# Preparation of a selective-scan kernel re-placed over 51 scan steps, a first tile with homes of its own, and identity matmuls ahead of the scans

## What is computed

```python
deltaBC = einsum('bld,od->blo', x, W_bc)          # x is normalised
dt_r, Bm, Cm = deltaBC[..., :64], deltaBC[..., 64:96], deltaBC[..., 96:]
delta = softplus(einsum('blr,dr->bld', dt_r, W_dt) + b_dt)
def step(h, inp):                                  # over 1024 time steps
    dA  = exp(delta_t[:, :, None] * A[None])       # A = -exp(A_log)
    dBu = (delta_t * u_t)[:, :, None] * B_t[:, None, :]
    h   = dA * h + dBu                             # h: (batch 4, 256, state 32)
    y_t = einsum('bdn,bn->bd', h, C_t)
y = scan(step) + u * D_param
```

## Time and profile before

| | us |
|---|---|
| median of 3 runs | 1049.39 (1044.85 to 1049.46) |
| the profiled execution | 1052.26 |
| its span, first to last instruction | 1050.3 |
| mean granted TensorE clock in it | 0.807 |

### The profile page before, as it was taken

How to read it: one execution, slowest core, us unless ns; L and a number is a source line. 1 busy time by engine, 2 the same in 40 slices (tenths; PEclk the granted TensorE clock), 3 DMA queues, 4 the chain that set the end, 5 groups by cost and what they waited for, 6 DMA issues and landing times.

```text
span 1050.3 us, 22285 instructions
## 1 busy us (share of the span) xinstructions
PE 868.0 (83%) x7468; PEld 633.2 (60%) x7468; DVE 767.9 (73%) x774; ACT 507.6 (48%) x897; POOL 459.7 (44%) x779
## 2 busy tenths in 40 slices
PE   5324798599979997899789978999999987999994
PEld 3114566466657665666566655666666655787883
DVE  7602697578657865786579658868999994889884
ACT  3451376347534753474347435754555514454441
POOL 6530435254425442545243525444333462555634
PEclk9655698869666967696669668967999978999998
DMA  7869356734663467356734573466646535210011
GB/s 297 92 132 145 52 104 90 157 54 96 89 151 58 96 81 157 60 96 86 148 61 99 81 156 59 102 87 144 95 96 99 112 96 148 63 61 21 21 41 61
DMA packets 234658, 103.59 MB, mean 99 GB/s; under 512 B 168112, under 2 KB 226992, under 8 KB 234160
## 3 DMA queue, kind: packets, MB, share of 16 engines
q1 hardware_dynamic: 234112, 95.80, 48.4%
q10 hardware_dynamic: 432, 6.29, 1.4%
HBM read 58.43 MB, written 43.61 MB: 97 GB/s over the span
## 4 chain that ended last, share of the span: by engine, by line
PE 39%; issue 25%; DVE 14%; POOL 7%; SPq 6%; ACT 5%; DMA 2%; ACTq 0%; POOLq 0%; DVEq 0%
DVE arena L1755 9%; PE psum L1339 7%; PE psum L1400 7%; PE psum L1407 7%; PE psum L1327 7%; PE psum L428 5%; PE psum L1260 2%; POOL arena L369 2%; POOL carry L1210 2%; SPq L945 1%; ACT arena L1558 1%; POOL arena L360 1%; SPq L970 1%; SPq L924 1%; PE psum L497 1%
## 5 line engine op out<-in xcount | busy, mean ns | idle before, releaser
L1755 DVE TENSOR_TENSOR_SCAN arena<-arena,psum 128x1024 f32<-128x1024 f32 x256 | 573.2, 2276 | 195.0 <-PE psum L1407 169.4
L1558 ACT ACTIVATE arena<-psum 128x512 f32<-128x512 f32 x512 | 278.3, 596 | 372.1 <-PE psum L1327 371.2
L1400 PEld LDWEIGHTS psum<-du_mov,b_sta 96*128 96x128 bf16 x2048 | 150.9, 113 | 205.0 <-DVE arena L1755 102.0
L1400 PE MATMUL psum<-du_mov,b_sta 96*128 96x128 bf16 x2048 | 193.5, 250 | 50.7 <-issue 25.0
L1407 PE MATMUL psum<-carry,ident 128*128 128x32 f32 x1024 | 182.6, 307 | 55.1 <-POOL carry L1210 55.0
L1327 PE MATMUL psum<-delta_mov,a_sta 96*128 96x128 bf16 x2048 | 195.1, 249 | 22.3 <-ACT arena L1558 15.2
L1407 PEld LDWEIGHTS psum<-carry,ident 128*128 128x128 f32 x1024 | 167.8, 233 | 61.0 <-POOL carry L1210 61.0
L1210 POOL TENSOR_TENSOR carry<-arena 128x64 f32<-128x64 f32 x252 | 109.6, 435 | 202.0 <-ACT arena L1558 140.6
L1327 PEld LDWEIGHTS psum<-delta_mov,a_sta 96*128 96x128 bf16 x2048 | 173.6, 125 | 27.3 <-ACT arena L1558 18.6
L1339 PE MATMUL psum<-arena,c_sta 128*32 128x512 f32 x1024 | 179.1, 775 | 0.0
L428 PE MATMUL psum<-delta_mov,arena 128*128 128x256 f32 (+6 forms) x544 | 114.6, 368 | 7.2 <-ACT arena L549 7.1
(11 more groups left out here) (167 smaller groups left out, 792.5 us busy)
## 6 DMA issues: line engine op xcount, KB each, us to landing
du_terms<-arena SPq DMA_DIRECT2D x24, 512.0 KB, 6.2
du_mov<-du_terms SPq DMA_DIRECT2D x128, 96.0 KB
du_mov<-du_terms SPq DMA_DIRECT2D x128, 64.0 KB
y<-y_rows SPq DMA_DIRECT2D x32, 256.0 KB
b_terms<-delta_mov ACTq DMA_DIRECT2D x3, 2048.0 KB, 12.4
delta_mov<-delta_terms SPq DMA_DIRECT2D x128, 48.0 KB
b_sta<-b_terms SPq DMA_DIRECT2D x128, 48.0 KB
delta_terms<-arena SPq DMA_DIRECT2D x46, 128.0 KB, 5.2
```

Source lines behind the costliest of these rows:

```text
L1400: mm = nc.tensor.matmul(sub(psum, 0, P, o, (2, 2), (TS, GD // 2), (1, 2)), b_sta[k][0:ROWS, (s * 4 + tg) * P:(s * 4 + tg + 1) * P], sub(du ...
L1558: nc.scalar.activation(sub(arena, 0, P, u * 16 * TS, (TS, 16), (decay_at(k, 1), SUBS), (1, TS)), sub(psum, 0, P, (4 + u % 2) * BANK, (TC, ...
L1755: nc.vector.tensor_tensor_scan(arena[:, STATE_AT[s] + o:STATE_AT[s] + o + GD * TS], arena[:, decay_at(k, s) + o:decay_at(k, s) + o + GD * TS],
```

## The change

- The preparation of tile p is cut in an early piece, run in tile p-2 (`early_piece`, n=10 to 30), a late piece, run in tile p-1 (`late_piece`, n=0 to 19), and the transposition of C at the start of tile p itself (`own_piece`). So only tile 0 is prepared before the first scan, with the front of tile 1 as far as z; tile 1's late piece runs in tile 0. There are late pieces in tiles 0 to 6 and early ones in 0 to 5. The loop is still over tiles 1 to 5.
- All tiles but 0 use one set of homes (`NEW = 1`); tile 0 has slots of its own that chunk 1's decay only needs later (`first_homes_free`).
- z: four matmuls of 512 columns at n = 24, 26, 28, 30. B and C: eight matmuls with x as the stationary operand give B already by time, so B needs no transposition and C gets one.
- The splitting of du subtracts the short copy (`u_short`) itself, on POOL at n=15 and 18.
- B's parts are padded with zeros in SBUF and stored as whole rows; the 6 MB zero fill of `b_terms` is gone. A is stored so that four loads replace sixteen.
- SP: delta is stored part by part, and chunk by chunk in tile 0, with new waits for the landing (`d_stored`, `uhi_stored`, ...); tile 0's du is stored from ACT's queue.
- Four units are prepared before the first scan instead of twelve (`units_at`).
- `spare`: matmuls of the identity on itself into a bank nobody reads: 12 before the weights are awaited, 4 behind W_eff, 6 behind each of six waits for the split of tile 0, and one behind each unit of the first chunk.

Its core; in order: the units by step, SP's queue, POOL's pieces, PE's, ACT's (`settle` lines are left out):

```diff
+def units_at(start, step):
+    if start and step < GROUPS - 1:
+        return [(0, (step + 1) * FIRST_UNITS + i) for i in range(FIRST_UNITS)]
+    if start and step == GROUPS - 1:
+        return [(1, i) for i in range(2 * UNITS_PER_STEP)]
+    at = (step - AHEAD) % STEPS * UNITS_PER_STEP
+    return [(int(step >= AHEAD), at + i) for i in range(UNITS_PER_STEP)]
...
+            if late and kk == 1:
+                p = lt + 1
+                sp_.wait_ge(S["dmid_ready"], p)
+                store_delta(p, 0)
+                store_delta(p, 1)
                 sp_.wait_ge(S["dlo_ready"], p)
+                store_delta(p, 2)
+                sp_.wait_ge(S["uhi_ready"], p)
+                store_du(p, NEW, 0, "uhi_stored")
+                sp_.wait_ge(S["d_stored"], 16 * D_STORES * p)
             if not (first and kk == 0):
                 store_y(c - 1)
+            if late and kk == 2:
+                p = lt + 1
                 sp_.wait_ge(S["ulo_ready"], p)
+                store_du(p, NEW, 2, "ulo_stored")
+                sp_.wait_ge(S["umid_ready"], p)
+                store_du(p, NEW, 1, "umid_stored")
+                store_b(p, NEW, "b_stored")
+            if early and kk == 3:
+                store_base(lt + 2, 1)
             if not (last and kk >= 2):
                 sp_.wait_ge(S["b_ready"], (c + 1) * STEPS)
+                if kk == 2:
+                    for done, stores in (("uhi_stored", 1), ("umid_stored", 1), ("ulo_stored", 1),
+                                         ("b_stored", TERMS)):
+                        sp_.wait_ge(S[done], 16 * stores * (lt + 1))
                 load_mu(c + 2, k)
...
+    def early_piece(p, n, first):
+        if n == 14:
             if first:
                 pool.wait_ge(S["first_xn"], 2)
             else:
                 pool.wait_ge(S["xn_ready"], p - 2)
+            rstds(p, NEW)
+        if n == 26:
             pool.wait_ge(S["xn_ready"], p - 1)
+            pool.wait_ge(S["xnT_psum"], 2 * p + 2)
+            base_product(p, NEW, xn[NEW])
+        if n == 27:
+            base_sum(p, NEW, xn[NEW])
+    def late_piece(p, n):
+        if n == 4:
+            b_rest(p, NEW)
+        if n == 7:
+            pool.wait_ge(S["sp_ln"], p + 1)
+            pool.tensor_tensor(delta[NEW], delta[NEW], sp[NEW], ALU.add).then_inc(S["delta_ready"], 1)
         if n == 8:
+            pool.wait_ge(S["delta_ready"], p)
+            pool.tensor_tensor(duT[NEW], delta[NEW], xnT[NEW], ALU.mult).then_inc(S["du_ready"], 1)
+        if n == 9:
+            b_low(p, NEW)
+        if n == 10:
+            pool.wait_ge(S["du_ready"], p)
+            pool.wait_ge(S["dhi_ready"], p)
+            pool.tensor_tensor(delta[NEW], delta[NEW], dparts[NEW][0], ALU.subtract).then_inc(S["dres_ready"], 1)
+        if n == 13:
+            pool.wait_ge(S["dmid_ready"], p)
+            pool.tensor_tensor(dparts[NEW][2], delta[NEW], dparts[NEW][1], ALU.subtract)\
+                .then_inc(S["dlo_ready"], 1)
+        if n == 15:
+            pool.wait_ge(S["u_short"], 2 * p - 1)
+            pool.tensor_tensor(du[NEW], du[NEW], u_short[NEW], ALU.subtract).then_inc(S["ures_ready"], 1)
         if n == 18:
+            pool.wait_ge(S["u_short"], 2 * p)
+            pool.tensor_tensor(du[NEW], du[NEW], u_short[NEW], ALU.subtract).then_inc(S["ulo_ready"], 1)
...
+    def spare(n, at):
+        for i in range(n):
+            nc.tensor.matmul(bank(at)[:, 0:P], ident[:, :], ident[:, :], start=True, stop=True)
     pe.wait_ge(S["ident_ready"], 1)
+    spare(12, 3)
...
+    for made in ("dmid", "dlo", "uhi", "ures", "umid", "ulo"):
+        pe.wait_ge(S["first_parts"], FIRST[made])
+        spare(6, 0)
...
+    def late_piece(p, n):
+        if n == 0:
+            pe.wait_ge(S["z_taken"], 2 * p + 2)
+            cb_products(NEW, 7)
+        if n in (8, 10):
+            r = (n - 8) // 2
+            if r == 0:
+                pe.wait_ge(S["bhi_ready"], p + 1)
+                pe.wait_ge(S["du_ready"], p)
+            else:
+                pe.wait_ge(S["duT_taken"], 2 * p + 1)
+            du_transposes(NEW, r, 7)
+    def early_piece(p, n):
+        if n == 20:
             pe.wait_ge(S["duT_taken"], 2 * p)
             pe.wait_ge(S["xn_ready"], p - 1)
+            xn_transposes(NEW, 0, 7)
+        if n == 22:
             pe.wait_ge(S["xnT_ready"], 2 * p + 1)
+            xn_transposes(NEW, 1, 7)
+        if n in (24, 26, 28, 30):
+            half, h = (n - 24) // 4, (n - 24) // 2 % 2
+            if half == 0 and h == 0:
                 pe.wait_ge(S["xnT_ready"], 2 * p + 2)
+            if half == 1 and h == 0:
                 pe.wait_ge(S["z_taken"], 2 * p + 1)
+            mm = z_mul(NEW, half, 7, h)
+            if h == 1:
                 mm.then_inc(S["z_psum"], 1)
...
+    def late_piece(p, n, first):
+        if n == 1:
+            if not first:
+                act.wait_ge(S["b_stored"], 16 * TERMS * (p - 1))
+            take_cb(p, NEW, 7)
+            exp_part(p, NEW)
+            ln_part(p, NEW)
         if n == 5:
+            b_middle(p, NEW)
         if n == 7:
+            act.wait_ge(S["delta_ready"], p)
+            if not first:
+                act.wait_ge(S["umid_stored"], 16 * (p - 1))
+                act.wait_ge(S["ulo_stored"], 16 * (p - 1))
+            nc.scalar.copy(dparts[NEW][0], delta[NEW]).then_inc(S["dhi_ready"], 1)
+        if n == 8:
+            take_du(p, NEW, 0, 7)
+        if n == 9:
+            act.wait_ge(S["dres_ready"], p)
+            nc.scalar.copy(dparts[NEW][1], delta[NEW]).then_inc(S["dmid_ready"], 1)
+        if n == 10:
+            take_du(p, NEW, 1, 7)
         if n == 11:
+            act.wait_ge(S["duT_taken"], 2 * p + 2)
+            nc.scalar.copy(u_short[NEW], du[NEW]).then_inc(S["u_short"], 1)
+        if n == 12:
+            act.wait_ge(S["u_short"], 2 * p - 1)
+            act.wait_ge(S["dlo_ready"], p)
+            nc.scalar.copy(uparts[NEW][0], u_short[NEW]).then_inc(S["uhi_ready"], 1)
+        if n == 14:
+            act.wait_ge(S["ures_ready"], p)
+            act.wait_ge(S["uhi_ready"], p)
+            nc.scalar.copy(u_short[NEW], du[NEW]).then_inc(S["u_short"], 1)
+        if n == 19:
+            act.wait_ge(S["u_short"], 2 * p)
+            act.wait_ge(S["d_stored"], 16 * D_STORES * p)
+            nc.scalar.copy(uparts[NEW][1], u_short[NEW]).then_inc(S["umid_ready"], 1)
+    def early_piece(p, n):
+        if n == 14:
+            normalise(p, 0)
+        if n == 15:
+            normalise(p, 1)
+        if n == 20:
+            act.wait_ge(S["umid_ready"], p - 1)
+            act.wait_ge(S["ulo_ready"], p - 1)
+            take_xnT(p, NEW, 0, 7)
+        if n == 22:
+            act.wait_ge(S["d_stored"], 16 * D_STORES * (p - 1))
+            take_xnT(p, NEW, 1, 7)
+        if n == 26:
             act.wait_ge(S["base_ready"], p + 1)
+            act.wait_ge(S["uhi_stored"], 16 * (p - 1))
+            take_z(p, NEW, 0, 7)
+        if n == 30:
+            take_z(p, NEW, 1, 7)
+    for u in range(FIRST_UNITS):
         exps(0, 0, u)
```

647 lines of the change are left out of this document (274 added, 373 removed).

## The result

| | before | after |
|---|---|---|
| median (four runs of each) | 1049.2 us | 1023.9 us (1010.1 to 1035.9) |
| profiled execution | 1052.3 | 1019.9 |
| its span | 1050.3 | 1018.1 |
| mean granted clock in it | 0.807 | 0.794 |

The ratio after to before is 0.968, 95% interval 0.959 to 0.977. The change makes the kernel 3% faster, where I had forecast 10%: 940 us, with a range that ended at 995. Two parts of the forecast nearly came, the head and a shorter tile 0. The third, tiles 1 to 6, hardly came: they took 595 us before and take 592.

What follows compares the result with a forecast made beforehand. Order of work bounds the kernel: 256 serial DVE scans, slowed where PE's waits drop TensorE to 1.2 GHz. Head, tiles and tail (57 + 91.5 + 4 x 92.2 + 85.8 + 77.8 + 70 + 190.2) gave 941, so 940 us; range 910 to 975, 8-in-10 868 to 995.

Steps and rivals of the forecast that it cites:

- head: Time before the first scan: 57 us, against 84.1 before; range 53 to 62.
- tile 0: First tile: 91.5 us, with a slow start of 35.4 and no wait for x at its third scan.
- tiles 1 to 6: Tiles with preparation beside scans: 92.2 us each for tiles 1 to 4, 85.8 for tile 5, 77.8 for tile 6.
- 5 us for landing: Last part of the head: du and B loads, issued by 50, land 5 us later; 2 more for PE.
- First chunk: Scans n=0 to 7 of a tile: kept at 29.7 us, small gains eaten by a second fall of the level.
- Second chunk: Scans n=8 to 15: 17.4 at the scans' pace plus 2.2 for statistics and shift, 19.6 us.
- Third chunk: Scans n=16 to 23: ACT's block and POOL's pieces leave, PE's idle time hides most additions; 17.6 us.
- rival (b): One more clock fall at n=10 behind the statistics in tiles 0 to 5: 32 us more, 972; chance 0.12.
- Fourth chunk: Scans n=24 to 31: 17.4 plus 1.5 for z products plus 6.4 for the loop's turn, 25.3 us.
- turn of the loop: At the loop's back edge, DVE's idle time stays as before: 6.4 us in each of tiles 1 to 4.
- rival (c): SP's queue becomes the bound and tiles 1 to 5 stay at 105.8 us: 1035 in all; chance 0.10.
- Tile 6: Holds tile 7's late part, whose ACT block costs 8.1 us over a clean tile: 77.8 us.

Runs made afterwards that it cites:

- a_nospare: Changed kernel without any of its multiplications of the identity; 1023.2 us, ratio 0.962 to the kernel before.
- a_again: The changed kernel itself, run once more as the measure for the others; 1015.1 us, ratio 0.967 to the kernel before.
- a_fill: Changed kernel with eight identity multiplications added ahead of step 3's exponents in a late tile and eight at the end of step 11; 999.2 us.
- a_nostat: Changed kernel with the statistics of tiles 2 to 7 left out; 1007.8 us, ratio 0.956 to the kernel before.
- a_all: Changed kernel with tile loop written out, sixteen identity multiplications added in TensorE's waits, and no statistics for tiles 2 to 7; 975.7 us.
- a_nob: a_all with SP storing only one of B's six terms for tiles 1 to 7; 953.3 us, ratio 0.900 to the kernel before.
- a_best2: a_best with B's six stores of a streamed tile issued by GpSimd instead of SP; 967.9 us, ratio 0.917 to the kernel before.
- a_best: Changed kernel, nothing left out: loop written out, eight identity multiplications at step 3 of a late tile, statistics spread over steps 8 to 13; 1000.8 us.
- a_fillstat: Changed kernel with both the sixteen added identity multiplications and no statistics for tiles 2 to 7; 998.7 us.
- a_noload: Changed kernel with the softplus logarithm replaced by an exponential, so no table is loaded; 997.0 us, ratio 0.944 to the kernel before.
- a_unroll: Changed kernel with the loop over tiles 1 to 5 written out; 991.0 us, ratio 0.942 to the kernel before.
- a_best3: a_best2 with the logarithm at step 3 instead of 1 and du stores ahead of the third chunk's delta loads; 952.4 us, ratio 0.913 to before.
- a_keep: Changed kernel with three identity multiplications added at each of steps 4 to 7 of a late tile; 1041.6 us, ratio 0.972 to the kernel before.

## Why the prediction was wrong, step by step

- **Head: right in its order, 6.5 us off, half of it in one term.** The delta stores ended at 38.1 (forecast 35.5), B at 43.0 (40), delta loads at 47.3 (44), du and B loads at 53.1 (50), then PE's first step came at 61.5. So 3.1 us were lost by the end of SP's issues, most of them in the delta stores, and 3.4 in "5 us for landing", which took 8.4. SP's timeline and PE's:

```profile
26.41 11.70 SPq L962 DMA_DIRECT2D delta_terms<-arena  x12
38.21 4.76 SPq L957 DMA_DIRECT2D b_terms<-arena  x6
43.07 4.18 SPq L982 DMA_DIRECT2D delta_mov<-delta_terms  x12
47.35 4.14 SPq L991 DMA_DIRECT2D du_mov<-du_terms  x12
51.53 1.61 SPq L997 DMA_DIRECT2D b_sta<-b_terms  x4
```

```profile
61.51 1.01 PE L1431 MATMUL psum<-du_mov,b_sta 96*128 96x128 bf16 x8 [10.21 <-DMA b_sta<-b_terms]
```

  The identity multiplications, counted at nothing, are worth nothing (a_nospare).
- **Tile 0: 91.5 forecast, 98.0 measured, 112.1 in a_again.** By chunks 36.1, 24.2, 17.4 and 20.4 for 35.4, 19.6, 17.6 and 18.9: the slow start was right, though with luck, since a_again has 40.2, 27.4, 25.7 and 18.8 there. The second chunk fails as below.
- **First chunk: 29.7 forecast, 31.2 to 32.3 measured in tiles 1 to 4 (25.8 to 32.3 in a_again).** ACT's block was 5.4 us (371.98 to 377.38) for 5.9, the wait 2.26 for 2.6. The B and C products were mis-sized: 1.9 against 3.62 (365.06 to 368.68), as all of them fell at 1.2 GHz.
- **Second chunk: 19.6 forecast, 22.4 to 27.4 measured, 19.1 us too few over tiles 1 to 4.** This is the first of the two steps that failed. I had let the fall at n=3 cost something inside the first chunk, as 13.5 us at 0.50 in the earlier trace rows had, and priced the second at clock 1.00. The stretch went on for 34 us (278.2 to 312.3, 377.1 to 411.3) and ran through it. That the kernel before showed 13.6 to 13.7 us at L1327 in five tiles held for that place alone: behind its turn at 303 it had one of 34.1. a_again has the chunk at 20.4 to 24.3, so this term moves from run to run. a_fill, which keeps every cause but PE's idleness at n=3, has it at 20.4 to 22.7.
- **Third chunk: 17.6 forecast, 17.4 in tiles 2 and 3, 25.5 and 29.1 in tiles 1 and 4, 29.1 in tile 5.** This is the other step that failed, by 19.0 us over tiles 1 to 4. Where there was no fall behind the statistics, the term was exact. Where there was one, rival (b) had it, priced at 5.3 us a tile; it cost 8 to 12, as it lasts 34 to 41 us and not two pairs of scans. a_nostat confirms its cause: without the statistics, third chunks took 17.4. The rule of the Trainium skill cited there (TensorE: Matmul & The Clock Gate, "HAM oscillation — how this bites in real kernels": a fall at each wait inside the loop) agrees with all but one of the 13 waits, though the level often came back long before the next.
- **Fourth chunk: 25.3 forecast, 21.0 to 25.3 measured.** Right in size, wrong in reason. Its 6.4 us "turn of the loop" was 2.3 to 6.1, and at two of the four turns it ended with B's landing behind SP's queue (a_all, a_nob and a_best2 show the queue at work). So rival (c) was true as a mechanism, at a smaller price: it had 95 us over the forecast, and the runs give 22 (a_all to a_nob) to 30 (a_best to a_best2), and it takes back part of a gain made earlier in the tile, as a_fillstat showed.
- **Tile 6: 87.0 for 77.8 (94.5 in a_again).** Its chunks were 23.7, 17.4, 22.5 and 23.4. The third and the fourth were to run at the scans' pace, and SP's queue delayed both. ACT stood 4.52 us for the landing of y, which SP had issued at 712.44 behind 10.37 us of delta stores, and PE 3.59 for ACT; at the turn to tile 7 PE waits 5.70 us for B. ACT's timeline and PE's:

```profile
719.94 0.59 ACT L1571 COPY y_rows<-psum 128x512 f32<-128x512 f32 x1 [4.52 <-DMA y<-y_rows]
```

```profile
721.08 1.10 PE L1349 MATMUL psum<-delta_mov,a_sta 96*128 96x128 bf16 x8 [3.59 <-ACT arena L1564]
```

The sum was linear: gains in chunks, added up. The measured kernel has two couplings that the sum lacked. A wait costs its own length and then the lower level behind it; and part of the time won in one chunk is waited for at the next landing. By the medians, against 1015.1, removing one cause gave 7 to 24 us each time (a_nostat 7, a_fill 16, a_noload 18, a_unroll 24). a_nostat, a_fill and a_unroll together, as a_all, gave 39, less than their 47. The whole kernel with SP's queue relieved as well gave 63 (a_best3).

The fall of the level behind idleness (a_fill, a_nostat) and SP's share at the turn (a_nob) are shown by runs. Why one stretch lasts 10 us and the next at the same place 34, with PE busy nearly throughout, is not settled, so the size of the two failed terms stays open.

## What to carry to other kernels

Count PE's waits, not its busy share: a wait of 2 us can be followed by 34 us at the lower level, and multiplications into an unread bank in its place can pay (16 us here, though one wait in each tile was left open). Before a gain is added to the next one, ask which queue was hidden behind the time just saved, and sum its issues over a tile at the new pace. A stretch at the lower level should enter a sum with the spread over all places and traces at hand: five equal rows from one place said nothing of the next place.

## What the runs showed of the hardware

- The return of the level scatters. Stretches at 1.2 GHz, with PE hardly idle in them, lasted from 3 to 41 us (after), and in four traces one of 78 to 89 lies over tiles 6 and 7 (a_fillstat 88.7, a_keep 81.9, a_nob 78.5, a_best2 78.5; PE busy for 88.2 of the 88.7). The total of one kernel scatters with it: a_nob took 944.7 us at a mean granted clock of 0.890 and 977.8 at 0.854.
- SP issued the twelve du loads ahead of the turn more slowly inside the loop (4.76 to 5.12 us, after) than written out (4.15 or 4.16, a_unroll), with pauses of 0.25 against 0.10 us between groups. B's six stores show no such difference: 7.46 to 8.35 us in the loop, 7.38 to 8.80 written out.
- In one execution of a_best PE ran at a third of its speed from start to end: eight scans took 52.9 us and not 17.4, the records grant it 1.00 all the same, and DVE's scans kept their 2287 ns:

```profile
PE 2478.3 (99%) x7516; PEld 1662.8 (66%) x7516; DVE 765.2 (31%) x768; ACT 541.0 (22%) x897; POOL 454.3 (18%) x781
...
L1361 PE MATMUL psum<-arena,c_sta 128*32 128x512 f32 x1024 | 419.5, 1714 | 0.0
```

A pair of scans is then 13.2 us, where it is 4.4 at 2.4 GHz and 7.0 at 1.2. The Trainium skill (TensorE: Matmul & The Clock Gate, "Seeing it yourself", the HAM trace caveats) tells of a clock stuck at a quarter, and warns not to trust each event. The row would fit a level below 1.2 GHz that the record doesn't show, but one execution proves no cause.
